# The first blocks of an attention: instructions rewritten, queues reordered, and the first scores computed twice

## The reference, cut to what matters

```python
x = _layernorm(x + _L0_gnn_ref(x, adj, adj, W1, f1, W2, f2))   # four passes of adj @ ...
x = _layernorm(x + _L1_gnn_ref(x, adj, beta))                  # attention, below
x = _layernorm(x + _L2_gnn_ref(x, adj, ...))                   # one pass of adj @ x, then a GRU
x = _layernorm(x + _L3_gnn_ref(x, adj, W_self, W_neigh))       # one pass of adj @ x

def _L1_gnn_ref(x, adj, beta):
    norm2 = jnp.linalg.norm(x, axis=1, keepdims=True)
    cos = beta * (x @ x.T) / (norm2 @ norm2.T + 1e-07)
    masked = cos + (1.0 - adj) * -1000000000.0
    P = jax.nn.softmax(masked, axis=1)
    return P @ x
```

## Time and profile before

| what | value |
| --- | --- |
| median of 3 runs | 1709.5 us (1707.4 to 1711.05) |
| the profiled execution | 1706.25 us |
| its span, first to last instruction | 1704.5 us |
| TensorE busy | 1648.2 us (97%) |
| VectorE busy | 1386.8 us (81%) |
| ScalarE busy | 1234.5 us (72%) |
| GpSimd busy | 232.1 us (14%) |
| mean granted clock of TensorE | 0.991 |

### The profile page before, as it was taken

One profiled execution on the slowest core, in us unless ns is written; L12 is line 12 of the kernel. 1 busy time (PEld: TensorE's weight loads), 2 busy tenths in 40 slices (PEclk: granted clock), 3 DMA queues, 4 the chain that ended last, 5 costly groups with the idle time before them and its releaser, 6 DMA issues.

```text
span 1704.5 us, 22279 instructions
## 1 busy us (share of the span) xinstructions
PE 1648.2 (97%) x8530; PEld 1378.2 (81%) x8530; DVE 1386.8 (81%) x1552; ACT 1234.5 (72%) x1255; POOL 232.1 (14%) x252
## 2 busy tenths in 40 slices
PE   7999999999999999977999999999999999999997
PEld 6788888888888888756999999999878867767886
DVE  6888888688768877877788788887888878788897
ACT  6777766576757766777778778877768768667776
POOL 0000000000000000137333333333440000000000
PEclk9999999999999999989999999999999999999999
DMA  9999999899989998981343333444369958849996
GB/s 392 372 363 365 386 336 375 285 388 353 362 296 379 362 356 293 331 323 56 144 149 139 128 135 144 149 149 149 137 245 348 354 193 279 285 150 319 330 328 205
DMA packets 86304, 461.61 MB, mean 271 GB/s; under 512 B 6672, under 2 KB 10928, under 8 KB 57648
## 3 DMA queue, kind: packets, MB, share of 16 engines
q1 hardware_dynamic: 86192, 460.14, 73.5%
HBM read 458.00 MB, written 2.11 MB: 270 GB/s over the span
## 4 chain that ended last, share of the span: by engine, by line
PE 81%; DVE 8%; ACT 4%; DMA 4%; issue 2%; POOL 1%; DVEq 0%; SPq 0%; ACTq 0%; POOLq 0%
PE ps L1237 17%; PE ps L1228 16%; PE ps L1231 16%; PE ps L1322 6%; DVE aL L822 5%; DMA raw<-adjT 4%; PE ps L1337 3%; PE ps L1307 3%; PE ps L1339 3%; PE ps L1309 3%; PE ps L1338 3%; PE ps L1308 3%; ACT aH L502 3%; PE ps L1267 1%; PE ps L1413 1%
## 5 line engine op out<-in xcount | busy, mean ns | idle before, releaser
L822 DVE TENSOR_TENSOR aL<-raw,aH 128x2048 fp32r<-128x2048 f32 (+1 forms) x364 | 826.0, 2274 | 166.3 <-ACT aH L502 163.0
L502 ACT ACTIVATE aH<-raw 128x2048 fp32r<-128x2048 f32 (+1 forms) x364 | 690.6, 1899 | 278.6 <-PE ps L1231 159.2
L1228 PE MATMUL ps<-aH,yH 128*128 128x512 f32 x1472 | 408.8, 400 | 10.0 <-ACT aH L502 9.9
L1237 PE MATMUL ps<-aL,yH 128*128 128x512 f32 x1472 | 399.6, 393 | 12.0 <-DVE aL L822 12.0
L1231 PE MATMUL ps<-aH,yL 128*128 128x512 f32 x1472 | 395.4, 390 | 0.0
L1237 PEld LDWEIGHTS ps<-aL,yH 128*128 128x128 f32 x1472 | 273.6, 188 | 81.8 <-DVE aL L822 26.3
L1228 PEld LDWEIGHTS ps<-aH,yH 128*128 128x128 f32 x1472 | 271.7, 189 | 72.4 <-issue 18.1
L1231 PEld LDWEIGHTS ps<-aH,yL 128*128 128x128 f32 x1472 | 276.6, 188 | 58.8
L1008 DVE TENSOR_TENSOR ptL<-ps,ptH 128x512 fp32r<-128x512 f32 x256 | 176.5, 689 | 83.1 <-ACT ptH L636 80.6
L636 ACT ACTIVATE ptH<-ps 128x512 fp32r<-128x512 f32 x192 | 114.2, 595 | 102.9 <-PE ps L1322 97.9
L1337 PE MATMUL ps<-ptH,yH 128*128 128x256 f32 x512 | 146.3, 286 | 10.1 <-DVE ptL L1008 9.2
(11 more groups left out here) (151 smaller groups left out, 1699.0 us busy)
## 6 DMA issues: line engine op xcount, KB each, us to landing
raw<-adjT SPq DMA_DIRECT2D x364, 1024.0 KB, 6.4
raw<-adj SPq DMA_DIRECT2D x28, 2048.0 KB, 8.1
raw<-adj SPq DMA_DIRECT2D x4, 1024.0 KB, 7.4
kept<-adj SPq DMA_DIRECT2D x2, 2048.0 KB, 13.9
kept<-adjT SPq DMA_DIRECT2D x4, 1024.0 KB, 12.6
xT<-norms SPq DMA_DIRECT2D x1, 2048.0 KB, 7.2
out<-xrow SPq DMA_DIRECT2D x8, 256.0 KB, 4.6
xrow<-x_rows SPq DMA_DIRECT2D x1, 1024.0 KB, 14.6
```

The costliest lines, as they stand in the source:

```text
L502: ins = nc.scalar.activation(a_tiles(q, t)[0][:, cols], a_source(q, t)[:, cols], ACT.Copy)
L822: ins = dve.tensor_tensor(low[:, cols], a_source(q, t)[:, cols], high.bitcast(F32)[:, cols], ALU.subtract)
L1228: pe.matmul(b, block(yH, k), high[:, c], start=(k == 0), stop=False)
L1237: ins = pe.matmul(b, block(yH, k), low[:, c], start=False, stop=(k == NB - 1))
```

## The change

Seven edits, all near the attention's beginning:

1. In `scale_step`, five `tensor_scalar` instructions (and one copy) on small tensors become `scalar_tensor_tensor`, which has a second tensor as input: the same tensor again, or a new constant tensor `eps`. The same for the four instructions that make the unit rows of chunk 6.
2. The product `epsu` leaves `scale_step` and is made once, for all blocks, behind the unit rows of chunk 6.
3. TensorE computes the first four calls of scores in a first pass that signals nothing, and then again as before.
4. `unit_low(6)` and `unit_low(7)` go ahead of mask steps 0 and 1 on VectorE.
5. On ScalarE the copy of `x` chunk 0 goes ahead of exponent 0 of row block 1, and exponents 1 to 3 go into steps 0, 2 and 4 of the first superblock.
6. GpSimd normalises chunks 0 to 3 (before: 0 to 4), chunk 2 earlier; VectorE normalises 4 to 7, at steps 0, 2, 4 and 6.
7. GpSimd's low parts 3 and up follow the last mask step.

```diff
-    X1_BY_POOL = 5
+    X1_BY_POOL = 4
...
+        eps = sb("eps", [D, 1])
...
             mask_bias(0, 1, 0, 3)
+            normalise(1, 2)
             mask_bias(0, 1, 1, 4)
             pool.wait_ge(unitL_ready, BK)
             stage_unit(1, 0)
             for h in range(2):
                 mask_bias(1, 0, h, 5 + h)
             low_of_x(4, 0)
-            normalise(1, 2)
             low_of_x(4, 1)
+            normalise(1, 3)
             stage_unit(1, 1)
+            mask_bias(1, 1, 0, 7)
             low_of_x(4, 2)
-            mask_bias(1, 1, 0, 7)
-            normalise(1, 3)
             mask_bias(1, 1, 1, 8)
-            low_of_x(4, 3)
-            normalise(1, 4)
-            for c in range(HBK, BK):
+            for c in range(HBK - 1, BK):
                 low_of_x(4, c)
...
+                    if not before and k in (0, 2, 4):
+                        exponent(1, 1, 1 + k // 2)
...
-            for r in range(2):
-                for c in range(NCH):
-                    exponent(r, r, c)
-                    if r == 1 and c in (0, 2):
-                        high_of_x(1, c // 2)
+            for c in range(NCH):
+                exponent(0, 0, c)
+            high_of_x(1, 0)
+            exponent(1, 1, 0)
+            high_of_x(1, 1)
             super_block(0, 0, 2, False)
...
-                    dve.tensor_scalar(mean[:, lo:hi], m, 0.5, None, ALU.mult)
-                    dve.tensor_scalar(v, raw_m2, 1.0 / D, LN_EPS, ALU.mult, ALU.add)
+                    dve.scalar_tensor_tensor(out=mean[:, lo:hi], in0=m, scalar=-0.5, in1=m, op0=ALU.mult, op1=ALU.add)
+                    dve.scalar_tensor_tensor(out=v, in0=raw_m2, scalar=1.0 / D, in1=eps[:, 0:1].to_broadcast([D, hi - lo]),
+                                             op0=ALU.mult, op1=ALU.add)
...
-                    dve.tensor_scalar(epsu[:, lo:hi], unorm[:, lo:hi], COS_EPS, None, ALU.mult)
-                    dve.tensor_copy(rstd[:, lo:hi], s3[:, 0, lo:hi])
+                    dve.scalar_tensor_tensor(out=rstd[:, lo:hi], in0=s3[:, 0, lo:hi], scalar=1.0, in1=s3[:, 0, lo:hi],
+                                             op0=ALU.mult, op1=ALU.max)
...
+            count(dve.memset(eps[:], LN_EPS))
...
-                ins = dve.tensor_scalar(unit_rows[HBK - 2][:, b % BPB * D:(b % BPB + 1) * D], block(xrow, b),
-                                        mean[:, b:b + 1], s3[:, 1, b:b + 1], ALU.subtract, ALU.mult)
+                ins = dve.scalar_tensor_tensor(out=unit_rows[HBK - 2][:, b % BPB * D:(b % BPB + 1) * D], in0=block(xrow, b),
+                                               scalar=mean[:, b:b + 1], in1=s3[:, 1, b:b + 1].to_broadcast([D, D]),
+                                               op0=ALU.subtract, op1=ALU.mult)
             ins.then_inc(unit_by_dve, 1)
+            count(dve.scalar_tensor_tensor(out=epsu[:], in0=unorm[:], scalar=COS_EPS, in1=unorm[:], op0=ALU.mult, op1=ALU.min))
...
-                    if not before and k in (2, 4, 6):
-                        x_rows_1(X1_BY_POOL + k // 2 - 1)
+                    if not before and k in (0, 2, 4, 6):
+                        x_rows_1(X1_BY_POOL + k // 2)
...
             for m in range(2 * NCH):
-                mask_chunk(0, m)
                 if m < QB:
                     unit_low(HBK + QB + m)
+                mask_chunk(0, m)
...
-                if j == CH // BANK - 1:
+                if j == CH // BANK - 1 and not again:
                     ins.then_inc(s_ready, 1)
...
             for q in range(HBK):
                 if q % 2 == 0:
                     project(3, HBK + QB + q // 2, None)
+                scores(0, q, True)
+            for q in range(HBK):
                 scores(0, q)
```

More of the change, by code:

```diff
@@ L874, in scale_step @@
                     link(dve.scalar_tensor_tensor(out=n2, in0=d, scalar=float(D), in1=raw_m2, op0=ALU.mult, op1=ALU.add))
-                    dve.tensor_scalar(n2, n2, TINY, None, ALU.max)
+                    dve.scalar_tensor_tensor(out=n2, in0=n2, scalar=TINY, in1=n2, op0=ALU.max, op1=ALU.max)
                     dve.tensor_tensor(v, v, d, ALU.add).then_inc(var_ready, 1)
@@ L885, in scale_step @@
                 elif i == 6:
-                    count(dve.tensor_scalar(r, q, 0.5, None, ALU.mult))
+                    count(dve.scalar_tensor_tensor(out=r, in0=q, scalar=-0.5, in1=q, op0=ALU.mult, op1=ALU.add))
                 elif i == 7 and norms_too:
@@ L1293, in _, with scores @@
                                 unit_turn(c)
-            def scores(sbi, q):
+            def scores(sbi, q, again=False):
                 m, j = divmod(q, CH // BANK)
```

## The result

The changed kernel took 1704.66 us at the median of 20 runs (1698.97 to 1711.7), the kernel before 1710.45 us at the median of 20 runs of its own (1705.44 to 1715.95). The ratio is 0.9971, 95% interval 0.996 to 0.9981: the change saves 0.29%, 5.0 us of 1710 (3.2 to 6.8). The plain difference of the two medians is 5.8 us. The forecast was 1705.0 us, from 1709.5.

What follows compares the result with a forecast made beforehand. TensorE was taken to bound the kernel from 830 us, so only the attention's beginning counted. +0.4 - 5.5 + 0.6 = -4.5 us gave 1701.75 for the profiled execution, 1705.0 us as median; range 1699.5 to 1709.7.

Steps and rivals of the forecast that it cites:

- What bounds: Attention from 830 us: TensorE alone limits, 1.84 us a step, so the rest of the kernel inherits the beginning's gain.
- Part 1: Last scales: instructions rewritten with two tensor inputs stay held by GpSimd, and the moved epsilon product nets zero; gain 0.
- part 5: GpSimd's chunk of x moved to VectorE: VectorE 0.6 to 1.7 us late at four steps; GpSimd's earlier chunk 2 costs 0.
- Rival B: Rewritten instructions pass GpSimd, so scales and rows come earlier: -8.5 us, 1701.0 us; chance 0.20.
- Part 2: First four blocks of scores done twice: cost 0 inside TensorE's idle time; clock benefit 0 to 2.4 us, taken as 0.
- Part 3: VectorE's low part before the mask: first mask step 0.7 to 0.9 us later, half regained, +0.4 at the first turns.
- Parts 4 and 5: First block, ScalarE's new order and the chunk of x moved from GpSimd to VectorE: 30.2 us for 35.76, -5.5 us.
- the walk: Step-by-step count of ScalarE's work through the first block's twelve steps, giving 30.2 us and a 3.9 us wait for wL.
- Rival C: VectorE bounds the first block: all four chunks of x at 2.82 us, +4.4 us, 1709.4 us; chance 0.20.
- rival D: First block runs at half clock from short TensorE stalls: 40.7 us instead of 35.76, 1714.8 us; chance 0.08.
- The restart behind the wait: Superblock 2's scores after the wait for wL: TensorE's half clock may last longer, +0.6 us (0 to 1.5).

Runs made afterwards that it cites:

- e4: Changed kernel with GpSimd's four superblock 0 mask steps moved behind the normalised chunks and VectorE's unit rows of chunk 6; ratio 0.9949 to the kernel before.
- e8: Changed kernel with GpSimd's four steps to superblock 2's row block 0 weights ahead of the low parts of x chunks 6 and 7; ratio 0.9941 to before.
- e5: Changed kernel with every rewritten VectorE instruction back in its one-input form (tensor_scalar or copy); ratio 0.9964 to the kernel before.
- e10: Changed kernel with VectorE's mask steps 0 and 1 again ahead of the low parts of chunks 6 and 7; ratio 0.9962 to the kernel before.
- e3: Changed kernel with the first four blocks of scores computed once instead of twice; ratio 0.9967 to the kernel before.
- e7: Against e4, the first four blocks of scores computed once instead of twice; ratio 0.9945 to the kernel before.
- e6: Changed kernel with the first four blocks of scores computed three times, the third behind the two small turns; ratio 0.9958 to the kernel before.
- e2: The kernel before, with only ScalarE's order taken from the change; ratio 0.9979 to the kernel before.
- e1: Changed kernel with ScalarE's old order, all four exponents of row block 1 ahead of the first superblock; ratio 0.9993 to the kernel before.

## Why the prediction was right

**What bounds.** Right: TensorE's steps beyond 830 us are 1.84 us in both kernels, and the gain of the beginning arrives at the end: 3.14 of 4.27 us in the pair of profiles, 8.96 of 9.18 in e4's against before. The stretches behind the attention differ by some tenths to nearly 2 us between executions (e8 kept 7.57 of 9.45).

**Part 1, the rewritten instructions: gain 0.** Right in mechanism, shown by e4 and e5. The price was not quite 0: the first mask step is 0.27 us later even in the old order (10.77 in e10 to 10.50), which holds the rows and the epsilon product. Of the rows' 2.92 us for 2.69 the new form can have at most 0.13, for in the old form (e5) they took 2.79; the rest comes with GpSimd's chunk 2, which now lies beside the last two and which part 5 put at 0. Rival B is refuted. One sentence was too wide: "two SBUF inputs are held just as one is" holds for `tensor_scalar`, but not for every instruction with one such input (L850 above).

**Part 2, the second pass: cost 0, benefit 0.** Right in the result: half clock at the third scores, and e3 and e7 with one pass are as fast. I gave two things as the reason, the idle stretch behind the pass and the few turns after it. The clock was still 1.00 over that idle stretch (3.54 us) and the two small turns, and 0.50 only from 757.75 on; which of the two brings the fall the runs do not tell. e6 has full clock at the third scores, so the benefit that I bounded at 2.4 us can be had (1.94 in one execution), but it takes a third pass.

**Part 3, the low part first: +0.7 to 0.9 us, half regained.** The first mask step moved by 0.89 and the first turns by 0.45 (e10). In sum the first turns are 0.87 us later where I had +0.4, inside the ends of 0 to 0.9; the rest is part 1's 0.27 and, as far as two executions can say, where the clock rises.

**Parts 4 and 5, the block: -5.5.** Measured -5.43, 30.33 us where the walk gave 30.2, and 3.41 us of wait for wL where it gave 3.9. But the working had this wrong in one respect: it put the whole gain under ScalarE's order and counted GpSimd's chunk as a price on VectorE alone. e2 and e1 show that ScalarE's order by itself gains 2.2 to 2.5 us in the profiles and that the rest by itself gains nothing. Of the other 3 us about half are waits of TensorE that go only with both; the rest is its busy time at the clock of the two executions. The walk came out right because it had both parts in it; that it did so within 0.2 us is partly luck, since the same block took 0.7 us less in e3, at a higher clock. It also missed where VectorE is late: one chunk at 4.08 us, above the 2.82 that I had as the upper end, and one wait of 2.38 us instead of four small ones. The four chunks took 1.17, 4.08, 1.66 and 1.11 us, 8.0 together for the 6.9 counted. Rival C took place in one step of four, rival D not: the clock over the block was 0.94.

**The restart behind the wait: +0.6.** Measured +0.29, between profiled executions that differ in the clock's rise by as much.

The terms measured sum to -4.27 against -4.5 and the runs give -5.0 (3.2 to 6.8), so the size was right too. That the time came within 0.4 us (1704.66 for 1705.0) is luck in part: the kernel before had 1710.45 us at its median of 20 runs, not 1709.5; and inside the sum the first turns were 0.47 us later than forecast and the restart 0.31 us cheaper.

## What to carry to other kernels

When VectorE and GpSimd run side by side, look at the ends: a VectorE instruction that is far longer than usual and ends within 0.02 us (128 x 8) to 0.14 us (128 x 128) of a long GpSimd one was held by it, and rewriting it with a second SBUF input doesn't free it; moving the long one does (3.55 us here). The price of such work depends on what it falls beside, not on its size: the same four rows took 1.11 to 6.64 us in these runs. When a queue's order is changed, ask what the moved work then waits for: in the profile ScalarE's new order was worth 2 us, and ScalarE then waited 6.1 us for GpSimd, until that was relieved too. And a wait that appears unchanged in both profiles, here 3.4 us for wL, can be worth as much as the whole change.

## What was not expected

A second pass of 2.8 us inside an idle stretch of 6.2 us moved the fall of the clock but not what it cost: 1.2 GHz (0.50) at the third scores in both, while with a third pass, placed behind two small turns, they had 2.4 GHz (1.00). And four VectorE instructions of 128 x 128 took 4.08 us beside a mask step and a low part of GpSimd, 3.7 times their undisturbed 1.11 us, and 6.64 us beside two of each in e1.
